# Banks, exponentials and order of the third layer's attention

## What is computed

```python
q, k, v = ((x @ W).reshape(B, T, nh, hd).transpose(0, 2, 1, 3) for W in (Wq, Wk, Wv))
attn = jnp.einsum('bhqd,bhkd->bhqk', q, k) / jnp.sqrt(hd) + bias[None, :, None, :]
masked = jnp.where(causal, attn, finfo.min)
probs = jax.nn.softmax(masked, axis=-1)
out = jnp.einsum('bhqk,bhkd->bhqd', probs, v).transpose(0, 2, 1, 3).reshape(B, T, C) @ Wo
```

## Time and profile before

| | us |
|---|---|
| median of 3 runs (2314.17 to 2317.09) | 2316.44 |
| the profiled execution | 2314.24 |
| its span | 2312.5 |
| TensorE busy | 2062.4 (89%) |
| VectorE busy | 1623.5 (70%) |
| ScalarE busy | 1283.3 (55%) |
| third layer's attention, first matmul to last division | about 460 |

### The profile page before, as it was taken

How to read it: one execution, slowest core, us unless ns; L and a number is a source line. 1 busy time by engine, 2 the same in 40 slices (tenths; PEclk the granted TensorE clock), 3 DMA queues, 4 the chain that set the end, 5 groups by cost and what they waited for, 6 DMA issues and landing times. The chain is left out here.

```text
span 2312.5 us, 56820 instructions
## 1 busy us (share of the span) xinstructions
PE 2062.4 (89%) x22888; PEld 1391.5 (60%) x22888; DVE 1623.5 (70%) x4129; ACT 1283.3 (55%) x2560; POOL 947.6 (41%) x1176
## 2 busy tenths in 40 slices
PE   4679998998999999999999796899999986889886
PEld 2448887996888887888887664344433333334233
DVE  7666664775666676667665563899898936698895
ACT  2247775565777777777776242267676763323323
POOL 2037776664678744665443032111111100154462
PEclk8789999999999999999999797699999997999998
DMA  6311113104011100000000063011111101000000
GB/s 180 106 64 38 39 38 97 50 29 149 21 39 19 35 3 20 2 21 3 3 2 2 16 205 106 16 43 49 38 37 38 40 4 38 0 0 9 0 9 19
DMA packets 77925, 94.14 MB, mean 41 GB/s; under 512 B 10145, under 2 KB 56242, under 8 KB 76002
## 3 DMA queue, kind: packets, MB, share of 16 engines
q1 hardware_dynamic: 64178, 77.23, 11.1%
q0 software_dynamic: 13488, 13.28, 2.9%
HBM read 54.55 MB, written 35.53 MB: 39 GB/s over the span
## 5 line engine op out<-in xcount | busy, mean ns | idle before, releaser
L1166 DVE TENSOR_REDUCE a_parts<-a_S 128x1 f32<-128x512 f32 (+1 forms) x576 | 363.0, 684 | 29.0 <-PE a_S L1050 22.7
L1137 ACT ACTIVATE WA<-a_E 128x1024 f32<-128x1024 f32 (+1 forms) x320 | 283.1, 940 | 117.9 <-PE a_E L1078 58.8
L1042 PE MATMUL a_S<-a_KS,a_QS 54*128 54x512 bf16 (+3 forms) x768 | 189.6, 348 | 31.0 <-DVE a_parts L1166 18.4
L463 POOL TENSOR_SCALAR WA<-WA,a1b_rinv 128x1024 f32<-128x1024 f32 (+3 forms) x192 | 142.5, 761 | 181.8 <-DVE a1b_rinv L802 181.6
L463 POOL TENSOR_SCALAR XR<-XR,a1b_rinv 128x768 f32<-128x768 f32 (+3 forms) x192 | 141.7, 752 | 118.9 <-DVE a1b_rinv L802 118.4
L618 PE MATMUL a1b_O<-a1b_PT,WA 128*64 128x128 f32 x3072 | 189.0, 276 | 0.0
L618 PEld LDWEIGHTS a1b_O<-a1b_PT,WA 128*64 128x64 f32 x3072 | 165.8, 137 | 6.5
L583 PE MATMUL a1b_B<-a1b_Kf,a1b_Qf 64*128 64x512 f32 (+2 forms) x768 | 156.2, 481 | 8.5 <-issue 4.6
L1042 PEld LDWEIGHTS a_S<-a_KS,a_QS 54*128 54x128 bf16 x768 | 58.7, 95 | 172.5 <-DVE a_parts L1166 136.0
L1090 PE MATMUL a_O<-WA,V 128*9 128x512 f32 (+3 forms) x1536 | 154.2, 489 | 0.1
L714 ACT ACTIVATE WA<-WA,a1b_nmax 128x1024 f32<-128x1024 f32 (+3 forms) x192 | 150.4, 792 | 1.3 <-DVE a1b_nmax L784 1.3
(11 more groups left out here) (533 smaller groups left out, 5890.9 us busy)
## 6 DMA issues: line engine op xcount, KB each, us to landing
WA<-in_w SPq DMA_DIRECT2D x8, 1024.0 KB, 9.0
a_QS<-qstack SPq DMA_DIRECT2D x32, 216.0 KB
a_KS<-kstack SPq DMA_DIRECT2D x32, 216.0 KB
a1b_tb<-tab SPq DMA_DIRECT2D x12, 512.0 KB
qstack<-f_parts SPq DMA_DIRECT2D x24, 256.0 KB
kstack<-f_parts SPq DMA_DIRECT2D x24, 256.0 KB
f_slots<-f1r_zrows SPq DMA_DIRECT2D x9, 516.0 KB
f1t_xs<-f_slots SPq DMA_DIRECT2D x9, 516.0 KB, 7.3
```

What stands on the lines that cost most here:

```text
L463: pool.tensor_scalar(v, v, rinv[:, e, u, part:part + 1], 1.0, ALU.mult, ALU.mult).then_inc(n_sb, 1)
L1042: ins = pe.matmul(pS[(at + half) % SB][:, lo:lo + n], QS[s][ROW[half], pair, i * P:(i + 1) * P], KS[s][ROW[half], pair, block * P:block * ...
L1137: act.activation(PT[q % NP][:, :, 0:w], pE[q % 2][:, :, 0:w], ACT.Exp).then_inc(e_sb, 1)
L1166: dve.tensor_reduce(peak, pS[at % SB][:, :].rearrange("p (c k) -> p c k", c=n), AX.X, ALU.max)\
```

## The change

The eight banks are dealt out anew: four for the ring of first scores (`SB` 4), three single ones in a ring for the second scores (`EB` 3), one for `pO`. The halves of second score q take ring places 2q and 2q+1 (counted over all iterations), modulo 3. Before its first matmul it waits for `e_sb` >= at + 2, where `e_sb` starts at 3: all exponentials up to the first half of score q - 1. ScalarE issues one ACTIVATE a half, both behind the one wait on `e_ps`. In a step the second pair of first scores moves from behind both second scores to between them.

```diff
-    SB = 3
+    SB, EB = 4, 3
-    pE = [ph.ps(f"E{i}", (P, 2, CH)) for i in range(2)]
+    pE = [ph.ps(f"E{i}") for i in range(EB)]
...
-                pe.wait_ge(e_sb, it * EQ + q + 1)
+                at = 2 * (it * EQ + q)
+                pe.wait_ge(e_sb, at + 2)
...
-                        ins = pe.matmul(pE[q % 2][:, half, lo:lo + n], KS[s][ROW[half], q % 2, j * P:(j + 1) * P],
+                        ins = pe.matmul(pE[(at + half) % EB][:, lo:lo + n], KS[s][ROW[half], q % 2, j * P:(j + 1) * P],
...
-                pe.wait_ge(e_sb, it * EQ + 2 * k + 4)
+                pe.wait_ge(e_sb, 2 * (it * EQ + 2 * k + 2) + EB)
...
                     second(it, 2 * n)
-                    second(it, 2 * n + 1)
                     if ahead(it, n, 1):
                         first(*ahead(it, n, 1))
+                    second(it, 2 * n + 1)
...
-                act.activation(PT[q % NP][:, :, 0:w], pE[q % 2][:, :, 0:w], ACT.Exp).then_inc(e_sb, 1)
+                for half in range(2):
+                    act.activation(PT[q % NP][:, half, 0:w], pE[(at + half) % EB][:, 0:w], ACT.Exp).then_inc(e_sb, 1)
...
-            act.sem_inc(e_sb, 2)
+            act.sem_inc(e_sb, EB)
```

More of the change, by code:

```diff
@@ L1077, in second @@
                                 rows, m = slice(half * HP, (half + 1) * HP), 1 + half - k
-                                ins = pe.matmul(pE[q % 2][:, half, lo:lo + (k + 1) * HP], units[rows, m * HP:m * HP + P],
+                                ins = pe.matmul(pE[(at + half) % EB][:, lo:lo + (k + 1) * HP], units[rows, m * HP:m * HP + P],
                                                 masks[rows, m, 0:(k + 1) * HP], start=False, stop=k == 1)
```

## The result

| | us |
|---|---|
| before, median of 4 (2314.17, 2316.44, 2317.09 and one of 4394.28) | 2316.77 |
| after the change, median of 4 (2342.12 to 2348.23) | 2342.69 |
| ratio | 1.0121, 95% interval 1.0100 to 1.0142 |
| profiled execution after, its span | 2348.23, 2346.5 |

One execution of the kernel before took 4394.28 us; why is not known, and the ratio is worked out without it.

The account below looks back on a forecast made before the run. VectorE was taken to bound the kernel before, the score-exponential chain after. Lead-in -4.7, first steps +1.9, 14 iterations +13.6, two late steps -0.2, run-out +7.0 gave +17.6 us: median 2334, range 2318 to 2346.

Parts of the forecast that it names:

- The signs: Trace marks named beforehand, among them over 100 TensorE waits for ScalarE, few for VectorE at L1042, period near 27.5 us.
- The hand-off of 0.85 us: Between second scores: 0.20 to ScalarE's start, 0.60 for a half's exponential, 0.05 to TensorE's next start.
- The step formula: Repeating part: first pair, second score, hand-off, second score and `weigh` add up; ten steps 27.4 us, 27.55 taken with weight loads.
- Run-out: Last 15 steps, without first scores: ScalarE no longer runs two scores ahead, 37.5 us against 30.5, +7.0.
- Lead-in: Before the first second score: the fourth bank removes VectorE's waits, -4.7 us, bounds -3.7 and -7.0.
- First three steps, low clock: Start of iteration 0, partly at the low clock and with the table load: 1.9 us more than the 9.8 before.
- The sum: Whole kernel: -4.7 + 1.9 + 13.6 - 0.2 + 7.0 = +17.6 us; the -0.2 is steps 3 and 4 of iteration 14.
- The ring's waits fall into the hand-offs: Repeating part: TensorE's waits for first-score banks are hidden while it waits for exponentials; VectorE needs 23.4 of 27.55 us.
- The shorter hand-off: Rival at the wait for half of score q - 1: hand-off 0.65 us, fourth bank wins, about 2304; chance 9%.
- the flat case: Rival of no change: period near 26.6 us, lead-in and run-out nearly cancel, +4, 2320; chance 9%.
- The one that put ScalarE at its limit: Rival: ScalarE becomes the bound if a half's exponential holds it 0.7 us, about 2355; chance 3%.
- The dear one: Rival: bank waits outlast the hand-off or `pO` copies delay more halves, 1 us more an iteration, 2349; chance 9%.

Follow-up runs that it names:

- e6: The change's kernel with each exponential covering only the first half of its columns, so its result is not the reference's; 2308.46 us.
- e1: The kernel before with only the exponentials split: three banks for first scores, four single ones for second scores, old order; 2314.62 us, ratio 1.0001.
- e8: The change's kernel with three banks for first scores instead of four, one bank left unused; 2369.05 us, ratio 1.0238.
- e2: The kernel before with split exponentials and the change's order in a step, three banks for first and four single ones for second scores; 2336.39 us, ratio 1.0094.
- e3: The change's kernel with the old order, both second scores side by side and then the second pair of first scores; 2374.96 us, ratio 1.0256.
- e4: The change's kernel with `weigh` between a step's two second scores and both pairs of first scores before the next; 2325.16 us, ratio 1.0047.

## Why the prediction held, and where it was short

- **What bounds the stage.** VectorE before, the chain of score and exponential after: right. The waits show the exchange, e6 shows the chain by shortening one link, and e1 clears the split.
- **The signs.** Met: 105 waits of TensorE for ScalarE, ScalarE's starts in pairs 0.49 apart, the first second score (32.3 us after the first maximum; 33.6 forecast). Not met: the waits for VectorE at L1042 fell to half (92.1 to 46.1 us in 320), not to a small part, though mostly under `weigh` or in the hand-off; VectorE's idle time is 4.7 us an iteration where about 4 were named.
- **The hand-off of 0.85 us.** Right to 0.01: 1.08 us from score to score in step 5, streaming included.
- **The step formula.** Mis-sized, the main miss. Steps 0 to 9 measured 2.53, 3.16, 3.12, 2.17, 2.98, 2.91, 3.19, 2.77, 3.05, 2.35, together 28.2 against 27.4. Eight of ten are 0.10 to 0.18 longer than listed. Steps 1 and 4 are 0.08 and 0.15 shorter: in step 4 the copy of `pO` began 0.54 us into the step (1549.79 to 1550.33), not 0.68, and held ScalarE 0.46, not 0.6, so that the first exponential began at 1.00, not 1.28. The mis-sized term is "a matmul that had to wait also shows part of its weight load ... at 0.03 for each step". It is 0.10. The row was to be had in the trace of before: a first score that had waited, unmasked, and the `weigh` behind it:

```profile
1595.81 0.09 PEld L1042 LDWEIGHTS a_S<-a_KS,a_QS 54*128 54x128 bf16 x1 [0.51 <-DVE a_parts L1166]
1596.13 0.12 PEld L1090 LDWEIGHTS a_O<-WA,V 128*9 128x9 f32 x8 [0.23 <-issue]
```

  0.32 us where streaming takes 0.22. The period grew by 1.65 us, not 0.97: 14 x 0.68 = 9.5 us of the miss. From step 3 of iteration 0 to step 3 of iteration 14 it is 395.3 us (1491.16 to 1886.50) against 372.0 (1488.31 to 1860.30), +23.3 for +13.6. The 256-column `weigh` took 0.55 (1549.24 to 1549.79), not 0.50.
- **Run-out.** +8.9 (39.4 against 30.5) for +7.0. The same 0.10 in each of 15 steps is 1.5 us, and the low clock, which the prediction did not expect there, 1.2. Together they are more than the 1.9 that is missing, so other terms of this part were 0.8 too high; which ones stays open.
- **Lead-in.** -6.0 for -4.7; the second scores began 5.8 us after the maxima rows, nearer the early bound of 4.4 than the 6.6 taken, and the rows themselves came after 26.6 us, not 27.1.
- **First three steps, low clock.** +2.0 for +1.9 (from the first second score to step 3, 1479.78 to 1491.16 against 1478.96 to 1488.31). The granted clock rose from 0.50 to 1.00 at about 1488.7, 8.9 us after the first second score, against 7.0 us in the kernel before.
- **The sum.** -6.0 + 2.0 + 23.3 - 0.2 + 8.9 = +28.0 of the measured +28.1. Against the 17.6 forecast, the iterations are 9.7 us over and the run-out 1.9; the lead-in takes 1.3 back, so part of the error is hidden by another. The time lies 3.3 us inside the upper end of the range.
- **"The ring's waits fall into the hand-offs".** Right for four banks: no PE row at L1042 waits for VectorE in the change, where the kernel before has 9.2 us of them. What the prediction did not see is that this is what the fourth bank does in the new order: e8 and e2 show 1.5 us an iteration lost without it. It took the order to be harmless in itself; it is not.
- **The rivals.** The shorter hand-off and the flat case fell with the 0.85. The one that put ScalarE at its limit fell with e1. The Trainium skill (ScalarE: Activation LUTs, Rules for kernel authors) states its 0.3 us for an ACTIVATE whose bias is a pointer operand. The exponentials here are given no bias, and 512 columns took 0.60 us and held ScalarE 0.49. The dear one, 1 us more an iteration, came nearest: the measured 2342.69 is 6.3 us from its 2349 and 8.7 from the forecast of 2334. The iterations did grow by 0.7 us more than forecast, though for the restart and not for a bank or a copy.

Still open: how the 1.5 us of e2 splits between the score behind the wait and its exponential arriving later. The rows of e1 and e2 give the first up to 1.8, but no run moved one without the other. Also untried: a wait for each half of a score by its own bank. The first half of score q goes into the bank that the second half of q - 2 has left, yet both halves wait for the first exponential of q - 1.

## What to carry to other kernels

Three single banks for scores that come in pairs hold one and a half scores. Each score then waits for the exponential just ahead of it, and each hand-off costs its whole length, from the last streamed column through the exponential to the next score, though no engine is busy all the time. Whether waits written for each bank would win some of it back, no run here shows. Ask first when a buffer is needed: here the fourth bank was worth 5 us in a stretch where it lay idle anyway, and could be lent there for nothing. When work is put into a gap, ask what now stands behind its own waits.

## What the runs showed of the hardware

- After a wait, TensorE loses 0.10 us once, beyond what it streams, whether a first or a second score had waited (`weigh` stood behind both): 0.32 for 0.22 (1595.81 to 1596.13 before the change, 1554.17 to 1554.49 after it).
- Exponentials of 256 columns took 0.38 us, of 512 0.60, and 512-column ones start 0.49 us apart, so splitting one of 1024 (0.91) added 0.07 us of ScalarE, and nothing to the time that e1 could tell.
- A copy between exponentials held ScalarE 0.46 us (1550.33 to 1550.79) where its record is 0.60.
- The granted clock fell to 0.50 in the run-out of the change (1908.6 to 1912, after TensorE had been busy 1.97 of 3 us) and of e3 (1943.1 to 1967); in those of the kernel before, e1, e2 and e4 it stayed at 1.00.
